# A feature-interaction tower on one Trainium2 core: the last gathered slot of the last tile handled apart from the five ahead of it

## What is computed

```python
e = jnp.stack([tbl_0[ids[:, 0]], ..., tbl_49[ids[:, 49]]], axis=1)      # 512 x 50 x 16
gram = jnp.einsum('bid,bjd->bij', e, e)
z = gram[:, _I_IDX, _J_IDX]                                             # upper triangle, 1225 columns
h = jnp.concatenate([z, dense_ctx], axis=1)                             # 1241 columns
h = jnp.maximum(h @ W_top1 + b_top1, 0.0)                               # 512 columns
h = jnp.maximum(h @ W_top2 + b_top2, 0.0)                               # 256 columns
y = h @ W_top3
```

## Time and profile before

| | us |
|---|---|
| median of 3 runs | 134.31 |
| lowest and highest run | 133.75, 134.50 |
| the profiled execution, device time | 134.14 |
| its span, first to last instruction | 132.3 |
| what lies around the span | 1.84 |
| busy in the span: PE, DVE, ACT, POOL | 116.3, 90.5, 73.1, 87.8 |
| mean granted clock of PE | 0.974 |

### The profile page before, as it was taken

One profiled execution on the slowest core, in us unless ns is written; L12 is line 12 of the kernel. 1 busy time (PEld: TensorE's weight loads), 2 busy tenths in 40 slices (PEclk: granted clock), 3 DMA queues, 4 the chain that ended last, 5 costly groups with the idle time before them and its releaser, 6 DMA issues.

```text
span 132.3 us, 3154 instructions
## 1 busy us (share of the span) xinstructions
PE 116.3 (88%) x1266; PEld 105.6 (80%) x1266; DVE 90.5 (68%) x162; ACT 73.1 (55%) x106; POOL 87.8 (66%) x96
## 2 busy tenths in 40 slices
PE   0199699739999999999989999999989999998990
PEld 0189486529996999999976999997789999898980
DVE  5947857997977789984875599965959635424211
ACT  7765999999699659964521934012930142222210
POOL 2777877877877778777777787787787787750000
PEclk9999999975699999999999999999999999999999
DMA  2999999993530100001011000000010000010000
GB/s 40 260 265 294 380 380 368 373 338 75 185 130 10 10 10 7 5 7 16 5 7 12 5 7 7 10 11 6 9 12 5 7 12 5 7 12 0 5 0 1
DMA packets 9411, 10.92 MB, mean 83 GB/s; under 512 B 2667, under 2 KB 6411, under 8 KB 9395
## 3 DMA queue, kind: packets, MB, share of 16 engines
q1 hardware_dynamic: 6453, 9.96, 22.8%
q0 software_dynamic: 2944, 0.76, 5.7%
HBM read 10.68 MB, written 0.03 MB: 81 GB/s over the span
## 4 chain that ended last, share of the span: by engine, by line
POOL 65%; issue 21%; PE 6%; DMA 3%; DVE 2%; POOLq 1%; DVEq 0%
POOL moving L317 33%; POOL moving L312 32%; DMA moving<-tbl,ids_sb 2%; PE psm L886 2%; PE gram L879 2%; DMA ids_sb<-in_ids 1%; PE pt L949 1%; POOLq L104 1%; DVE blocks L222 1%; PE p L886 1%; PE gram L886 1%; DVE mcols L659 0%; DVE h2w L704 0%; DVEq L667 0%; DVEq L653 0%
## 5 line engine op out<-in xcount | busy, mean ns | idle before, releaser
L317 POOL DMA_INDIRECT moving<-tbl,ids_sb x48 | 45.6, 950 | 14.6 <-issue 14.6
L312 POOL DMA_INDIRECT moving<-tbl,ids_sb x44 | 41.9, 953 | 15.5 <-issue 13.1
L886 PE MATMUL p<-z,w_sb 128*128 128x128 f32 x312 | 38.7, 275 | 0.0
L834 PE MATMUL psm<-table,onehot 128*128 128x160 f32 (+1 forms) x208 | 34.6, 317 | 3.9 <-DVE picked L588 3.3
L886 PEld LDWEIGHTS p<-z,w_sb 128*128 128x128 f32 x312 | 37.0, 192 | 0.8 <-issue 0.4
L834 PEld LDWEIGHTS psm<-table,onehot 128*128 128x128 f32 x208 | 30.6, 208 | 6.2 <-DVE picked L588 4.5
L577 DVE TENSOR_REDUCE fixed<-picked 128x48 f32<-128x480 f32 (+2 forms) x32 | 19.7, 635 | 0.2
L237 DVE COPY z<-gram 63x384 f32<-63x384 f32 (+1 forms) x18 | 9.3, 516 | 10.9 <-PE gram L879 6.8
L588 DVE TENSOR_TENSOR picked<-psm,mask_more 128x480 f32<-128x480 f32 x20 | 13.0, 651 | 5.0 <-PE psm L834 4.8
L222 ACT COPY blocks<-mcols 32x384 f32<-32x384 f32 (+3 forms) x15 | 13.0, 863 | 3.7 <-DVE mcols L659 3.5
L237 ACT COPY z<-gram 63x384 f32<-63x384 f32 (+1 forms) x18 | 7.8, 434 | 12.6 <-PE gram L879 10.0
(11 more groups left out here) (58 smaller groups left out, 102.7 us busy)
## 6 DMA issues: line engine op xcount, KB each, us to landing
w_sb<-in_w SPq DMA_DIRECT2D x12, 256.0 KB
wide<-quotients SPq DMA_DIRECT2D x9, 320.0 KB, 6.6
moving<-tbl,ids_sb POOLq DMA_INDIRECT x92, 2.4
table<-in_small SPq DMA_DIRECT2D x5, 240.0 KB, 3.6
table_big<-in_big SPq DMA_DIRECT2D x4, 200.0 KB
table<-in_small SPq DMA_DIRECT2D x2, 256.0 KB, 4.9
w_sb<-in_w SPq DMA_DIRECT2D x1, 512.0 KB, 10.0
table<-in_small SPq DMA_DIRECT2D x1, 192.0 KB, 5.1
```

Source lines behind the costliest of these rows:

```text
L312: nc.gpsimd.indirect_dma_start(moving[:, t, YS + n, 0:D], None, tables[n - 1], bass.IndirectOffsetOnAxis(ap=large_ids[:, t, n:n + 1], axis=0),
L317: nc.gpsimd.indirect_dma_start(moving[:, t, XS + n, 0:D], None, tables[HALF + n - 1], bass.IndirectOffsetOnAxis(ap=large_ids[:, t, HALF + ...
L834: ins = nc.tensor.matmul(psm[:, m % 2, START[f] - START[a]:START[f + 1] - START[a]], onehot[:, t % 2, f, :], table[:, START[f]:START[f + 1 ...
L886: return nc.tensor.matmul(hidden_sums(t, k), w1_sb[:, c, P * k:P * (k + 1)], z[:, t % 2, c, :], start=first, stop=last)
```

## The change

The late part of the last tile, the slots 7 to 12, is handled in two pieces instead of one: the slots 7 to 11, and slot 12. The gather of slot 12 has a semaphore of its own, `last_gathered`; `tail_gathered` counts the five others. DVE has a turn and three spread copies for each piece, ACT a spread copy for each piece, and one raise, of the slots 7 to 11, as before. PE has the same matmuls in the same order; its second `product_x` waits for three sets of spread copies instead of two. `piece(a)` gives the number of turns of this tile ahead of the one of slot a.

```diff
+        last_gathered = sem("last_gathered")
...
+        def piece(a):
+
+            return (a >= CUT) + (a == YS - 1)
+
...
                 for n in range(HALF):
+                    landed = late_gathered[t]
+                    if t == TILES - 1 and XS + n >= CUT:
+                        landed = tail_gathered if XS + n < YS - 1 else last_gathered
...
-                    ).then_inc(tail_gathered if t == TILES - 1 and XS + n >= CUT else late_gathered[t], 16)
+                    ).then_inc(landed, 16)
...
             def spread_late(t, a, b):
 
-                act.wait_ge(late_cols, t + (2 if a else 1))
+                act.wait_ge(late_cols, t + 1 + piece(a))
...
-            raise_late(3, CUT, YS)
-            spread_late(3, CUT, YS)
+            raise_late(3, CUT, YS - 1)
+            spread_late(3, CUT, YS - 1)
+            spread_late(3, YS - 1, YS)
             unload_x(3, CH - TAIL, CH)
...
             def turn_late(t, a, b):
 
                 dve.wait_ge(lower_placed, 2 * (t + 1))
-                if a:
+                if a == YS - 1:
+                    dve.wait_ge(last_gathered, 16)
+                elif a:
                     dve.wait_ge(tail_gathered, 16 * (b - a))
...
-            turn_late(3, CUT, YS)
-            spread_late(3, CUT, YS)
+            turn_late(3, CUT, YS - 1)
+            spread_late(3, CUT, YS - 1)
+            turn_late(3, YS - 1, YS)
+            spread_late(3, YS - 1, YS)
             unload_x(3, CH - TAIL, CH)
...
-                    pe.wait_ge(late_blocks[half], spread_by(half, t, 2 if a else 1))
+                    pe.wait_ge(late_blocks[half], spread_by(half, t, 3 if a else 1))
```

More of the change, by code:

```diff
@@ L664, in spread_late @@
                 dve.wait_ge(zeroed[t % 2], 2 - t % 2)
-                dve.wait_ge(late_cols, t + (2 if a else 1))
+                dve.wait_ge(late_cols, t + 1 + piece(a))
                 if t >= 2:
```

## The result

The changed kernel took 133.67 us in the median of 22 runs (133.21 to 134.14), the kernel before 134.09 us in the median of 22 (133.43 to 134.86). In a second comparison the same kernel gave 0.9952 (0.9934 to 0.9970).

The account below looks back on a forecast made before the run. The prediction took the path behind slot 12's gather, through DVE's turn and copies to PE's second product, as the bound. That start moves from 121.54 to 121.18, so 134.31 - 0.36 = 133.95 us; range 133.4 to 134.5.

Parts of the forecast that it names:

- The chain of reasons: Behind the last gather, DVE's turn and copies set PE's second product; a shift of its start shifts the end.
- DVE's first piece: On DVE, slots 7 to 11: turn from 118.41 after slot 11 lands, copies done at 119.93, before slot 12's turn.
- The small copies: DVE's three one-slot spread copies of slot 12: 165 ns each, 0.20 us apart, ending at 120.83.
- The prediction's estimate from that page: Skill page's 150 cycles, 156 ns fixed per copy instead of 132: six copies some 0.14 us later, gain about 0.22 us.
- the sum from rows: DVE's turns and copies priced by interpolating profile rows: second product starts at 121.18 instead of 121.54, gain 0.36 us.
- PE's floor: Earliest second product by PE's own list: 0.12 us after the bias matmul's start, at 121.03, capping the gain at 0.51 us.
- ACT at nothing: ACT's two spread copies cost nothing: the second ends at 120.45, 0.38 us ahead of DVE's last copy.
- B: Rival: slot 11 lands late and delays DVE's whole chain; 0.44 us slower, 134.75 us; chance 0.08.
- the decisive point: Rival of a late slot 11 decides once that slot is over 0.36 us late, a landing time over 2.76 us.
- A: Rival: slot 12's gather often lands later than in the trace; gain up to 0.83 us, 133.5 us; chance 0.17.
- C: Rival: small copies and turns on DVE as dear as the memsets or dearer; gain 0 to 0.2 us, 134.2; chance 0.15.
- PE's idle time would fall to nothing: Sign in the changed profile: PE's idle time before the second product falls from 0.36 us to nothing.

## Why the prediction was right

The forecast was 133.95 us, a gain of 0.36 us, "the same" within 0.5%. Measured: 133.67 us, and a gain of 0.42 between the medians of 22 runs each. 0.22 of the 0.28 us between forecast and measured time is the median of before, which fell from 134.31 to 134.09 with more runs.

- **The chain of reasons held.** The product's start is the end's start: shown by the 7.99 to 8.03 us behind it in every profile, and by the kernel that waits for all six slots, where 0.9 us in the profile are 0.9 to 1.0 us in the times. Slot 11's landing sets when slot 12 is turned: the turn of slot 12 followed the copy ahead of it after 0.02 to 0.04 us in every kernel with that cut but one. With the copies two and two the gap was 0.09 us; there DVE was done sooner, and slot 12 landed only about 2.4 us after its issue at 117.47, so it may have held the turn.
- **DVE's first piece.** Predicted start 118.41, copies to 119.93; measured 118.38 and 119.94. The turn of one slot, 234 ns predicted, took 0.24 us.
- **The small copies were mis-sized.** I took 165 ns each and 0.20 us apart; they took 192 ns (0.64 us for three), so 0.22 apart, and DVE ended at 120.94 instead of 120.83. The group of DVE's operations in the changed kernel:

```profile
L223 DVE COPY blocks<-mcols 32x160 f32<-32x160 f32 x3 | 0.9, 310 | 0.2
L223 DVE COPY blocks<-mcols 32x32 f32<-32x32 f32 x3 | 0.6, 192 | 0.2
```

  With 219 ns for 64 elements and 275 for 128 in the kernel that is cut after slot 10, the cost is no straight line down from 416 elements. The fixed part that shows at small sizes is about 160 ns, not 132. The trace of before had a third size that the prediction did not use, 400 ns where its line gives 365:

```profile
L222 DVE COPY blocks<-mcols 32x224 f32<-32x224 f32 x3 | 1.2, 400 | 0.2
```

  The rule of the Trainium skill ("VectorE: DVE Perf Modes", the TRN2 errata), with its fixed term of about 150 cycles at 0.96 GHz, 156 ns, and the 1.04 ns for an element of the earlier trace rows, gives an estimate of 156 + 33 = 189 ns for one slot: the trace agrees with it here (192). For five slots it gives 322, where 310 were measured. The prediction's estimate from that page for the whole, a gain of 0.22 us, is near the 0.26 us of the two first profiles, and the 0.36 of the sum from rows is what the two profiles of each kernel give in the mean. So the whole gain does not decide between the two prices; the copy of one slot does, for the page's.
- **PE's floor was mis-sized.** I read 0.12 us from a bias matmul with a second-layer matmul behind it; the pair products follow it after 0.20 to 0.21 us. The floor was 0.09 us later than I had it, and the most that this change could have given was 0.63 - 0.21 = 0.42 us in the profile, not 0.51. DVE still ended last, by 0.07 to 0.14 us. What the extra 0.09 us are was not tested.
- **ACT at nothing** was right: it ended 0.44 us ahead of DVE (I had 0.38), and undoing its part changed nothing that can be told.
- **Luck in the number.** The path forecast a start 4.03 us behind the last gather's issue instead of 4.39. Measured, in the mean of two profiles each, are 4.11 and 4.47: the new path was dearer by 0.08 us, for the small copies above all, and the old one too, for a last gather that came later in one profile. That the difference is again 0.36 is two equal errors.
- **The rivals.** B, a late slot 11, did not come: in the seven profiles that have the cut after slot 11 and wait for it alone, the first turn starts 2.38 to 2.53 us after that gather's issue, while the decisive point was 2.86 (2.76 and the 0.10 to the turn). A, a late slot 12, may be part of the gain: one of the two profiles near 134 us of the kernel before had it 0.15 us later. C, fixed costs that eat the gain, came in part, 0.1 us of it.
- **One reading would have misled.** I had said that PE's idle time would fall to nothing, and it did; the chain of waits then names PE. Leaving out DVE's copies moved the product by 0.13 to 0.17 us all the same.

## What to carry to other kernels

Where the last of several transfers is handled apart, the piece ahead of it should be done when the last one lands; otherwise the engine that works them off in order gives back part of the gain. Cut where the first piece's work fits into the gap between its landing and the last one: with a gather each 1.25 us and about 1.5 us of work for a piece, DVE was late for the last slot with the cut one slot ahead of the end, and waited for it with the cut two slots ahead. In the profile that was worth 0.14 to 0.18 us at the product, as much as PE's list let through; in the times it did not show. A cut further ahead was not run. And before pricing such a gain, look for the next path: here PE's own list was 0.4 us behind, and only moving both paths gave more than that in the profile.

## What the runs showed of the hardware

- Late gathers came back at the same places of the stream. Slot 10, issued near 114.7 (114.4 to 115.0), took 2.9 to 3.2 us in all eleven profiles near 134 us, where its neighbours took 2.2 to 2.6. It is the 90th of 92. In the first profile of the kernel before, from the 35th gather on, numbers 37, 46, 53, 64, 65, 75, 82 and 90 took 3.1 to 3.5 us, number 83 took 2.7, and all others 2.2 to 2.5. In five more profiles that were read through, of the kernel before, the changed one and two edited ones, numbers 65, 75 and 90 are late again (2.9 to 3.3 us), and one or two of 46 and 47 and of 82 to 84 (2.7 us and more). What causes it stays open. The slots 11 and 12 fell on none of these places in any of the eleven, and so rival B did not come.
- A busy row of a matmul (0.27 to 0.28 us for the bias) is longer than the time after which the next can start: 0.12 us with second-layer matmuls behind it, 0.20 to 0.21 with the small pair products. So PE's timeline can show no idle time although PE waited: 0.07 us above the floor in the changed kernel's first profile, and 0.14 us in its second, where the product starts 0.35 us behind the bias matmul and the row has no idle time either.
